# Expert rounds of four subtiles with a merged sixth chunk, transposes behind the down projection

## The chip, the cores and the metric

One core of a Trainium2 chip runs the whole kernel in float32. The metric is the device time of one launch in microseconds (us), the median of the runs shown. All other times come from one profiled execution of the kernel.

## The reference

The input is `x` of shape (8, 64, 16, 16): 8 images of 256 tokens with 64 channels. An attention block comes first, then a mixture of 8 experts in which each token uses two.

```python
x = x + conv_ref(ln_c(x))                  # kq = w_kq x + b, softmax(kq^T kq), w_o (attn v) + b_o
t = to_tokens(x)                           # 2048 tokens x 64 channels
f = ln_t(t)
probs = softmax(f @ router_w.T)            # 8 experts
gate, e = top_2(probs), renormalised
h = silu(f @ w1[e].T) * (f @ w3[e].T)      # w1, w3: 682 x 64
t = t + sum(gate * (h @ w2[e].T))          # w2: 64 x 682
```

## The kernel before, in words

**Attention.** The images go through TensorE (PE), ScalarE (ACT) and VectorE (DVE) one after another. Behind each image DVE chooses the two experts of each token, PE ranks the tokens within their expert (`rank`), and GpSimd (POOL) scatters normalised rows of 128 tokens to a list per expert in HBM (`scatter_row`, four indirect DMAs an image, 32 in all). `t_deviation(b + 1)`, two small POOL instructions that DVE's `normalise_t(b + 1)` needs, is issued ahead of the last row that POOL scatters in its loop turn for image b.

**Subtiles.** The lists are cut into 39 subtiles of 128 rows of one expert (`NS`). Which expert and which rows a subtile has is known only at run time: DVE works out a `table` in three phases (slots 0 to 7, 8 to 15, 16 to 38). Its pieces (`owners_of_slots`, `rows_of_slots`, `used_up`, `subtiles_of_experts`, `occupancy`) stand between DVE's multiplications of the first rounds, in an order written by hand (`tables_between`).

**Rounds.** A round has two subtiles (`HALVES`), so there are 20 rounds (`NT`). For each subtile SP reads expert and row number from the table into registers, and issues a load of the rows (`x_in`, 32.5 KB) and a load of the expert's weights (576 KB). Weights have 8 slots and rows 8. DVE copies rows into `x_pairs` (`pair_up`), PE transposes them (`turn_x`, L962) and ACT copies them to `x_cols` (`columns`). The 682 hidden units are 6 chunks of 128, the last one padded. One `up` step does two chunks: w1 in the upper 64 rows of the array (L982) and w3 in the lower (L984) side by side, into 512 columns of a PSUM bank each. ACT takes the Silu of the first (`silu`, L493), DVE multiplies (`multiply`, L798), and `down` (L1000) adds the six chunks up, the two subtiles in the two column halves of the array. `y_copy` (ACT), `turn_y` (PE, L1011) and `results` (DVE, L806) turn the outcome round, and POOL scatters it to HBM (`scatter_result`, L352).

**Order on PE** in a round i: two up steps, the transposes of the rows of round i + 1 and of the results of round i - 2, the third up step, and then the down steps of round i - 1. The down projection is thus one round behind. An `up` step g waits for `silu` g - 2 and `multiply` g - 3, because there are two banks for w1 and three for w3.

**Order on POOL**: 26 rows are scattered at once, the last six in pairs ahead of rounds 0 to 2, and results are scattered two or three in a round.

**The end.** When all 39 results have landed, they are loaded (`y_in`), weighted, added, transposed with the residual and stored.

Of the kernel before, what the change touches and what calls it, by code (L numbers as in the profile page):

```python
# [17 lines left out]
P = 128  # L18
# [12 lines left out]
HALVES = 2  # L31
PAIR = HALVES * SUB
CAP = B * N
NS = E + (K_TOP * CAP - 1) // SUB
NT = -(-NS // HALVES)
# [9 lines left out]
CHUNKS = -(-H // P)  # L45
HP = CHUNKS * P
WW = HP + CHUNKS * C
STEPS = CHUNKS // 2
PARK = K_TOP * CAP
YROWS = PARK + NS * SUB  # L50
WSLOTS = 8
XRING = 8
RING = 8
ROWS_AT_ONCE = TPB * K_TOP * 6 + 2
ROWS_OF_ROUND = (2, 2, 2)
assert ROWS_AT_ONCE + sum(ROWS_OF_ROUND) == TPB * K_TOP * B
HRING = 2 * STEPS
# [3 lines left out]
def metaformer(nc, x_tok, projections, value_output, b_o, experts, xs, ys, out):  # L61
    with ExitStack() as ctx:
# [6 lines left out]
        bank = [ctx.enter_context(nc.psum_tensor(f"bank{i}", [P, BLK], F32)) for i in range(8)]  # L69
# [78 lines left out]

        x_in = sb("x_in", [P, XRING, HALVES, RW])
        x_pairs = sb("x_pairs", [P, 2, HALVES, 2, C])  # L150
        x_cols = sb("x_cols", [P, 2, PAIR])
        act_sb = sb("act_sb", [P, 3, BLK])
        hid = sb("hid", [P, HRING, BLK])
        y_cols = sb("y_cols", [P, 2, P])
        y_out = sb("y_out", [P, RING, HALVES, C])
# [39 lines left out]
        x_paired, y_row_ready = sem("x_paired"), sem("y_row_ready")  # L195
# [12 lines left out]
        H1_BANK, H3_BANK, Y_BANK, X_BANK, R_BANK = bank[0:2], bank[2:5], bank[5], bank[6], bank[7]  # L208
        TABLES = 9 + PHASES
        CONST_DMAS = 3  # L210
        PER_TILE = 16 * HALVES

        def halves(i):
            return range(min(HALVES, NS - HALVES * i))

        def live(i, columns):
            n = len(halves(i))
            return columns.rearrange("p (c q) -> p c q", q=PAIR)[:, :, 0:n * SUB]
# [7 lines left out]
        def pairs_of(p):  # L226
            return range(-(-OPENED[p] // HALVES), -(-OPENED[p + 1] // HALVES))
# [7 lines left out]
        def all_scattered(engine):  # L235
            for r in range(RING):
                engine.wait_ge(y_scattered[r], 16 * sum(len(halves(i)) for i in range(r, NT, RING)))
# [13 lines left out]
        def _(sp):  # L251
# [12 lines left out]
            def load_weights(i, owners):  # L264
                if i >= WSLOTS // HALVES:
                    sp.wait_ge(hid_used, STEPS * (i - WSLOTS // HALVES + 1))
                for h in halves(i):
                    s = (HALVES * i + h) % WSLOTS
                    sp.dma_start(weights[:, s, :], experts[bass.ds(owners[h], 1)].rearrange("o p c -> p (o c)")
                                 ).then_inc(w_loaded[s], 16)  # L270

            def owners_of(i):
                return [sp.value_load(table[0:1, 0, HALVES * i + h:HALVES * i + h + 1], min_val=0, max_val=E - 1)
                        for h in halves(i)]

            def rows_of(i):
                return [sp.value_load(table[0:1, 1, HALVES * i + h:HALVES * i + h + 1], min_val=0, max_val=E * CAP - SUB)
                        for h in halves(i)]

            def load_rows(i, at):  # L280
                if i >= XRING:
                    sp.wait_ge(y_row_ready, i - XRING + 1)
                    sp.wait_ge(x_paired, i - XRING + 1)
                for h in halves(i):
                    sp.dma_start(x_in[:, i % XRING, h, :], xs[bass.ds(at[h], SUB), :]).then_inc(x_in_loaded[i % XRING], 16)
# [6 lines left out]
            early_rows = [rows_of(i) for i in range(2)]  # L292
            landed(0)
            for i in pairs_of(0):
                load_rows(i, early_rows[i] if i < 2 else rows_of(i))
                if i > 0:
                    load_weights(i, owners_of(i))
            for p in range(1, PHASES):
                sp.wait_ge(table_ready, p + 1)
                for i in pairs_of(p):  # L300
                    at = rows_of(i)
                    if i == pairs_of(p)[0]:
                        landed(p)
# [11 lines left out]
        def _(pool):  # L315
# [31 lines left out]
            def scatter_result(j):  # L347
                i, h = divmod(j, HALVES)
# [16 lines left out]
            nc.gpsimd.memset(ones[:], 1.0).then_inc(ones_made, 1)  # L365
            nc.gpsimd.memset(upto[:], 1.0).then_inc(ones_made, 1)
# [20 lines left out]
            rows_done, results_done = 0, 0  # L387
            for b in range(B):
                own = range(TPB * K_TOP * b, min(TPB * K_TOP * (b + 1), ROWS_AT_ONCE))
                for n in own:  # L390
# [3 lines left out]
                    rows_done += 1  # L394
            for i in range(NT):
                pool.wait_ge(h1_done, STEPS * i + 1)
                paced = i < len(ROWS_OF_ROUND)
                for n in range(ROWS_OF_ROUND[i] if paced else 0):
                    scatter_row(rows_done)
                    rows_done += 1  # L400
                for n in range(0 if paced else HALVES + i % 2):
                    if results_done < HALVES * (i - 1):
                        scatter_result(results_done)
                        results_done += 1
            for j in range(results_done, NS):
                scatter_result(j)

        @block.scalar
        def _(act):
# [71 lines left out]
            def columns(i):  # L481
# [3 lines left out]
                n = SUB * len(halves(i))  # L485
                nc.scalar.copy(x_cols[:, i % 2, 0:n], X_BANK[:, 0:n]).then_inc(x_cols_ready, 1)

            def silu(g):
                act.wait_ge(h1_done, g + 1)
                if g >= 3:  # L490
                    act.wait_ge(hid_done, g - 2)
                i = g // STEPS
                nc.scalar.activation(live(i, act_sb[:, g % 3, :]), live(i, H1_BANK[g % 2][:]), ACT.Silu  # L493
                                     ).then_inc(silu_done, 1)

            def y_copy(i):
                act.wait_ge(hid_used, STEPS * (i + 1))
                if i >= 2:
                    act.wait_ge(y_turned, i - 1)
                n = C * len(halves(i))  # L500
                nc.scalar.copy(y_cols[0:n, i % 2, :], Y_BANK[0:n, 0:P]).then_inc(y_copied, 1)  # L501

            columns(0)
            for i in range(NT):
                if i >= 2:
                    y_copy(i - 2)
                silu(STEPS * i)
                silu(STEPS * i + 1)
                if i + 1 < NT:
                    columns(i + 1)  # L510
                silu(STEPS * i + 2)
            y_copy(NT - 2)
            y_copy(NT - 1)
# [17 lines left out]
        def _(dve):  # L531
# [224 lines left out]
            def pair_up(i):  # L756
                slot, n = i % XRING, len(halves(i))
                dve.wait_ge(x_in_loaded[slot], PER_TILE * (i // XRING) + 16 * n)
# [4 lines left out]
                own = slice(HALVES * i, HALVES * i + n)  # L763
# [28 lines left out]
            def multiply(g):  # L792
                dve.wait_ge(silu_done, g + 1)
                dve.wait_ge(h3_done, g + 1)
                if g >= HRING:
                    dve.wait_ge(hid_used, g - HRING + 1)
                i = g // STEPS
                nc.vector.tensor_tensor(live(i, hid[:, g % HRING, :]), live(i, H3_BANK[g % 3][:]),  # L798
                                        live(i, act_sb[:, g % 3, :]), ALU.mult).then_inc(hid_done, 1)

            def results(i):
                dve.wait_ge(y_turned, i + 1)
                if i >= RING:
                    dve.wait_ge(y_scattered[i % RING], PER_TILE * (i // RING))
                n = len(halves(i))
# [3 lines left out]
            def tables_between(i, s):  # L809
                if (i, s) == (0, 0):  # L810
                    owners_of_slots(1)
                elif (i, s) == (0, 1):
                    rows_of_slots(1)
                elif (i, s) == (1, 1):
                    used_up(1)
                elif (i, s) == (1, 2):
                    subtiles_of_experts(2)
                elif (i, s) == (2, 1):
                    owners_of_slots(2)
                elif (i, s) == (3, 1):  # L820
                    rows_of_slots(2)
                elif (i, s) == (4, 1):
                    occupancy(2)
                elif (i, s) == (7, 1):
                    gate_shifts()

            for i in range(NT):
                for s in range(STEPS):
                    multiply(STEPS * i + s)
                    if s == 0 and i + 2 < NT:  # L830
                        pair_up(i + 2)
                    tables_between(i, s)
                if i >= 2:
                    results(i - 2)
            results(NT - 2)
            results(NT - 1)
# [13 lines left out]
        def _(pe):  # L850
# [104 lines left out]
            def turn_x(i):  # L955
# [5 lines left out]
                for h in halves(i):  # L961
# [3 lines left out]
            def up(g):  # L965
                i, s = divmod(g, STEPS)
                if s == 0:
                    pe.wait_ge(x_cols_ready, i + 1)
                    for h in halves(i):
                        j = HALVES * i + h  # L970
# [5 lines left out]
                for half in range(2):  # L976
                    at = P * (2 * s + half)
                    for h in halves(i):
                        slot = (HALVES * i + h) % WSLOTS
                        dst = slice(PAIR * half + SUB * h, PAIR * half + SUB * (h + 1))  # L980
                        src = slice(SUB * h, SUB * (h + 1))
                        first_ = nc.tensor.matmul(H1_BANK[g % 2][:, dst], weights[0:C, slot, at:at + P],  # L982
                                                  x_cols[0:C, i % 2, src], start=True, stop=True)
                        second_ = nc.tensor.matmul(H3_BANK[g % 3][:, dst], weights[C:P, slot, at:at + P],  # L984
                                                   x_cols[C:P, i % 2, src], start=True, stop=True)
                first_.then_inc(h1_done, 1)
                second_.then_inc(h3_done, 1)

            def down(g):
                i, s = divmod(g, STEPS)  # L990
                pe.wait_ge(hid_done, g + 1)
                if s == 0 and i >= 1:
                    pe.wait_ge(y_copied, i)
                for half in range(2):
                    chunk = 2 * s + half
                    at = HP + C * chunk
# [82 lines left out]
```

## Time and profile before

| what | value |
|---|---|
| median of 3 timed runs | 199.64 us (199.47 to 201.18) |
| span of the profiled execution | 204.1 us |
| PE busy | 174.5 us |
| DVE, POOL and ACT busy | 106.8, 85.5, 75.3 us |
| moved by DMA | 33.36 MB |

The page gives no other time for the profiled execution than its span from the first instruction to the last, 4.5 us above the median of the timed runs. The DMA share is the mean busy share of 16 engines. The first expert round begins on PE at 73.6 us, and the last down projection ends at 185.8 us.

### The profile page before, as it was taken

How to read it: one execution, taken by the hardware profiler on the slowest of the kernel's cores; microseconds unless marked ns; L12 is line 12 of the kernel's file. 1: busy time of each engine (PE TensorE's matmuls, PEld its weight loads, DVE VectorE, ACT ScalarE, POOL GpSimd, SP SyncE). 2: the span in 40 equal slices, each digit the busy share in tenths (PEclk: the TensorE clock that was granted, in tenths of full speed). 3: DMA queues.
4: the chain of work that ended last, by engine and by line, in shares of the span. 5: the costliest groups of instructions: out<-in, count | busy, mean ns of one | idle time of the engine just before them, and what ended most of it. 6: DMA issues, size and time to landing. Idle time of an engine off the chain costs nothing.

```text
span 204.1 us, 5200 instructions
## 1 busy us (share of the span) xinstructions
PE 174.5 (85%) x1744; PEld 141.7 (69%) x1744; DVE 106.8 (52%) x434; ACT 75.3 (37%) x172; POOL 85.5 (42%) x119
## 2 busy tenths in 40 slices
PE   1599989889899688799999999999999999949043
PEld 1254766756757577688888888888888888837032
DVE  4243345455676768956775554454444454612061
ACT  2255351532521611224444444444444444413002
POOL 3235017655666787403333333333333333553200
PEclk9999999999999999759999999999999999997958
DMA  3999000000045469507777887778878783000144
GB/s 73 324 300 248 0 0 20 16 13 28 8 101 178 140 189 305 189 18 257 256 261 250 263 265 259 262 261 261 270 253 265 260 258 116 13 29 6 53 165 103
DMA packets 21627, 33.36 MB, mean 163 GB/s; under 512 B 9810, under 2 KB 14962, under 8 KB 21602
## 3 DMA queue, kind: packets, MB, share of 16 engines
q1 hardware_dynamic: 18466, 29.90, 46.8%
q0 software_dynamic: 2272, 2.35, 3.5%
q10 hardware_dynamic: 864, 0.79, 1.2%
q8 instruction: 14, 0.23, 0.5%
q14 instruction: 11, 0.09, 0.1%
HBM read 25.90 MB, written 7.13 MB: 162 GB/s over the span
## 4 chain that ended last, share of the span: by engine, by line
PE 68%; POOL 8%; issue 8%; DVE 6%; DMA 4%; ACT 2%; POOLq 1%; SPq 1%; ACTq 0%; DVEq 0%
PE bank L982 26%; PE bank L1000 13%; PE bank L878 6%; POOL xs L343 4%; PE bank L899 4%; PE bank L869 4%; PE bank L863 3%; PE bank L962 3%; PE bank L888 2%; DMA y_in<-ys 2%; PE bank L1045 2%; POOL ys L352 2%; PE bank L984 2%; POOL rstd_t L333 1%; PE bank L856 1%
## 5 line engine op out<-in xcount | busy, mean ns | idle before, releaser
L982 PE MATMUL bank<-x_cols,weights 64*128 64x128 f32 x468 | 67.4, 293 | 1.9 <-DVE hid L798 1.9
L984 PE MATMUL bank<-x_cols,weights 64*128 64x128 f32 x468 | 67.5, 293 | 0.0
L982 PEld LDWEIGHTS bank<-x_cols,weights 64*128 64x128 f32 x468 | 59.0, 198 | 9.1 <-issue 7.2
L352 POOL DMA_INDIRECT ys<-y_out,y_row x39 | 37.3, 957 | 58.0 <-PE bank L982 39.5
L798 DVE TENSOR_TENSOR hid<-bank,act_sb 128x512 f32<-128x512 f32 (+1 forms) x60 | 40.5, 676 | 38.6 <-ACT act_sb L493 33.7
L984 PEld LDWEIGHTS bank<-x_cols,weights 64*128 64x128 f32 x468 | 59.0, 198 | 0.0
L493 ACT ACTIVATE act_sb<-bank 128x512 f32<-128x512 f32 (+1 forms) x60 | 35.1, 586 | 57.9 <-PE bank L982 57.5
L343 POOL DMA_INDIRECT xs<-xrows,pos x32 | 31.9, 998 | 22.0 <-issue 10.1
L1000 PE MATMUL bank<-hid,weights 128*64 128x128 f32 x468 | 32.9, 286 | 3.0 <-ACT y_cols L501 3.0
L1000 PEld LDWEIGHTS bank<-hid,weights 128*64 128x64 f32 x468 | 27.9, 143 | 5.6 <-issue 3.4
L899 PE MATMUL bank<-u_sb,probsT 128*128 128x73 f32 x64 | 15.6, 423 | 3.5 <-ACT probsT L446 3.5
L899 PEld LDWEIGHTS bank<-u_sb,probsT 128*128 128x128 f32 x64 | 14.3, 329 | 4.1 <-ACT probsT L446 4.1
L878 PE MATMUL bank<-kq 32*128 32x256 f32 x32 | 16.6, 670 | 0.0
L878 PEld LDWEIGHTS bank<-kq 32*128 32x128 f32 x32 | 9.3, 319 | 4.1 <-issue 1.9
L869 PEld LDWEIGHTS bank<-wu_x,xT 65*128 65x128 f32 x32 | 7.4, 321 | 6.0 <-issue 5.7
L1045 PE MATMUL bank<-ident,total_y 128*128 128x128 f32 x16 | 3.9, 423 | 8.0 <-DVE total_y L846 8.0
L962 PE MATMUL bank<-ident,x_pairs 128*128 128x128 f32 x39 | 9.4, 323 | 0.1
L564 DVE TENSOR_REDUCE neg_max<-bank 128x2 f32<-128x512 f32 x8 | 5.5, 691 | 7.4 <-PE bank L878 7.2
L1045 PEld LDWEIGHTS bank<-ident,total_y 128*128 128x128 f32 x16 | 3.3, 292 | 8.7 <-DVE total_y L846 8.3
L869 PE MATMUL bank<-wu_x,xT 65*128 65x81 f32 x32 | 9.1, 438 | 0.3 <-DVE wu_x L742 0.3
L863 PE MATMUL bank<-xT,proj 64*32 64x256 f32 x16 | 8.5, 631 | 1.0 <-ACT xT L421 1.0
L501 ACT COPY y_cols<-bank 128x128 f32<-128x128 f32 (+1 forms) x20 | 5.3, 263 | 10.8 <-PE bank L1000 6.9
(137 smaller groups left out, 182.1 us busy)
## 6 DMA issues: line engine op xcount, KB each, us to landing
weights<-experts SPq DMA_DIRECT2D x39, 576.0 KB
xs<-zeros SPq DMA_DIRECT2D x4, 1040.0 KB, 10.7
x_in<-xs SPq DMA_DIRECT2D x39, 32.5 KB, 2.8
ys<-y_out,y_row POOLq DMA_INDIRECT x39, 3.9
xs<-xrows,pos POOLq DMA_INDIRECT x32
y_in<-ys SPq DMA_DIRECT2D x2, 256.0 KB, 4.3
y_in<-ys ACTq DMA_DIRECT2D x2, 256.0 KB, 4.6
x_sb<-x_tok SPq DMA_DIRECT2D x1, 384.0 KB, 3.9
```

Of the source, the lines that this page charges most:

```text
L343: nc.gpsimd.indirect_dma_start(xs, bass.IndirectOffsetOnAxis(ap=pos[:, b, at:at + 1], axis=0), xrows[:, TPB * b + at // K_TOP, at % K_TOP, ...
L352: nc.gpsimd.indirect_dma_start(ys, bass.IndirectOffsetOnAxis(ap=y_row[:, j:j + 1], axis=0), y_out[:, i % RING, h, :], None).then_inc(y_sca ...
L493: nc.scalar.activation(live(i, act_sb[:, g % 3, :]), live(i, H1_BANK[g % 2][:]), ACT.Silu).then_inc(silu_done, 1)
L798: nc.vector.tensor_tensor(live(i, hid[:, g % HRING, :]), live(i, H3_BANK[g % 3][:]), live(i, act_sb[:, g % 3, :]), ALU.mult).then_inc(hid_ ...
L863: nc.tensor.matmul(K_BANK[0:CK, 0:N], wk, xT[0:C, b % 2, :], start=True, stop=True).then_inc(kq_done, 1)
L869: ins = nc.tensor.matmul(U_BANK[:, UX * i:UX * (i + 1)], xT[:, b % 2, P * i:P * (i + 1)], wu_x[:], start=True, stop=True)
L878: ins = nc.tensor.matmul(S_BANK[b % 2][:, N * i:N * (i + 1)], kq[:, b % 3, P * i:P * (i + 1)], kq[:, b % 3, :], start=True, stop=True)
L899: ins = nc.tensor.matmul(O_BANK[:, (TX + 1) * i:(TX + 1) * (i + 1)], probsT[:, b % 2, j, P * i:P * (i + 1)], u_sb[:, 2 * b + j, 0:TX + 1], ...
L962: ins = nc.tensor.transpose(X_BANK[:, P * h:P * (h + 1)], x_pairs[:, i % 2, h, :, :], ident[:])
L982: first_ = nc.tensor.matmul(H1_BANK[g % 2][:, dst], weights[0:C, slot, at:at + P], x_cols[0:C, i % 2, src], start=True, stop=True)
L984: second_ = nc.tensor.matmul(H3_BANK[g % 3][:, dst], weights[C:P, slot, at:at + P], x_cols[C:P, i % 2, src], start=True, stop=True)
L1000: ins = nc.tensor.matmul(Y_BANK[C * h:C * (h + 1), 0:P], weights[:, slot, at:at + C], hid[:, g % HRING, src], start=(chunk == 0), stop=(ch ...
```

## The change

- A round has four subtiles (`QUAD`): 10 rounds, the last of three subtiles. There are 12 weight slots (3 rounds) in place of 8 (4 rounds), and four deep rings of four for rows and results.
- An up step does one chunk for four subtiles. There are five full chunks and a sixth step for the 42 hidden units left: w3 and w1 of these lie side by side in one weight block of 106 columns, which stands in both row halves, so that one matmul a subtile computes both, for two subtiles at a time. Silu and multiplication of that step use 42 partitions, and the rest of `hid` is cleared by POOL at the start. The weights of a subtile have 1130 columns in place of 1152.
- On PE the down projection of a round follows its own up steps; behind it come the transposes of the results of the round before and of the rows two rounds ahead. In the last round the results of round 8 are transposed behind its first up step.
- `pair_up(i + 2)` stands behind the third multiplication of a round, `results(i - 2)` behind the first. The pieces of the table are spread over the steps of rounds 0 and 1.
- POOL scatters all 32 rows, then all results in order, with no pacing.

```diff
@@ pool
-                own = range(TPB * K_TOP * b, min(TPB * K_TOP * (b + 1), ROWS_AT_ONCE))
+                own = range(TPB * K_TOP * b, TPB * K_TOP * (b + 1))
                 for n in own:
                     if n == own[-1] and b + 1 < B:
                         t_deviation(b + 1)
                     scatter_row(n)
-            for i in range(NT):
-                pool.wait_ge(h1_done, STEPS * i + 1)
...
-            for j in range(results_done, NS):
+            for j in range(NS):
                 scatter_result(j)
@@ scalar
+                else:
+                    act.wait_ge(h3_done, g + 1)
+                    nc.scalar.activation(act_sb[0:TAIL, g % 3, :].rearrange("p (k n) -> p k n", k=2),
+                                         TAIL_BANKS[C:C + TAIL], ACT.Silu).then_inc(silu_done, 1)
...
             columns(0)
+            for i in range(NQ):
                 silu(STEPS * i)
+                if i == 0:
+                    columns(1)
+                for s in range(1, STEPS):
+                    silu(STEPS * i + s)
+                if i + 2 < NQ:
+                    columns(i + 2)
+                y_copy(i)
@@ vector
+            for i in range(NQ):
                 for s in range(STEPS):
                     multiply(STEPS * i + s)
+                    if s == 0 and i >= 2:
+                        results(i - 2)
+                    if s == 1 and i == NQ - 1:
+                        results(i - 1)
+                    if s == 2 and i + 2 < NQ:
                         pair_up(i + 2)
                     tables_between(i, s)
+            results(NQ - 1)
@@ tensor, up
+                    if s < FULL:
+                        first_ = nc.tensor.matmul(H1_BANK[g % 2][:, src], weights[0:C, slot, P * s:P * (s + 1)],
                                                   x_cols[0:C, i % 2, src], start=True, stop=True)
+                        second_ = nc.tensor.matmul(H3_BANK[g % 3][:, src], weights[C:P, slot, P * s:P * (s + 1)],
                                                    x_cols[C:P, i % 2, src], start=True, stop=True)
+                    else:
+                        rows_ = slice(C * (h % 2), C * (h % 2 + 1))
+                        ins = nc.tensor.matmul(TAIL_BANKS[0:TAIL_W, h % 2, SUB * (h // 2):SUB * (h // 2 + 1)],
+                                               weights[rows_, slot, TAIL_AT:TAIL_AT + TAIL_W], x_cols[rows_, i % 2, src],
+                                               start=True, stop=True)
@@ tensor, down and order
+                for s in range(STEPS):
+                    pe.wait_ge(hid_done, STEPS * i + s + 1)
+                    for h in members(i):
...
             turn_x(0)
             attend(B - 1)
+            for i in range(NQ):
+                up(STEPS * i)
+                if i == 0:
+                    rank(B - 1)
+                    pe.wait_ge(t_ready, B)
+                    turn_x(1)
+                if i == NQ - 1:
+                    turn_y(i - 1)
+                for s in range(1, STEPS):
+                    up(STEPS * i + s)
+                down(i)
+                if 1 <= i < NQ - 1:
+                    turn_y(i - 1)
+                if i + 2 < NQ:
+                    turn_x(i + 2)
+            turn_y(NQ - 1)
```

## Rows read from the trace of the kernel before

**Rows 1.** The page: busy time by engine; one group of DMA issues.

```profile
PE 174.5 (85%) x1744; PEld 141.7 (69%) x1744; DVE 106.8 (52%) x434; ACT 75.3 (37%) x172; POOL 85.5 (42%) x119
...
x_in<-xs SPq DMA_DIRECT2D x39, 32.5 KB, 2.8
```

**Rows 2.** Chain that ended last, by time: start us, us, what.

```profile
105.00 1.46 PE bank L1000 x24
106.46 0.30 PE bank L982
...
110.01 1.46 PE bank L1000 x24
```

**Rows 3.** PE timeline of a steady round: start us, us, instruction.

```profile
123.42 0.44 PE L962 MATMUL bank<-ident,x_pairs 128*128 128x128 f32 x2
...
123.90 0.37 PE L982 MATMUL bank<-x_cols,weights 64*128 64x128 f32 x1
...
124.11 0.27 PE L982 MATMUL bank<-x_cols,weights 64*128 64x128 f32 x1
...
124.78 0.27 PE L982 MATMUL bank<-x_cols,weights 64*128 64x128 f32 x1
...
124.99 1.53 PE L1000 MATMUL bank<-hid,weights 128*64 128x128 f32 x24
```

**Rows 4.** ACT timeline, steady rounds; in brackets idle time and its releaser.

```profile
95.76 0.60 ACT L493 ACTIVATE act_sb<-bank 128x512 f32<-128x512 f32 x1 [1.47 <-PE bank L982]
...
123.52 0.60 ACT L493 ACTIVATE act_sb<-bank 128x512 f32<-128x512 f32 x1 [0.30 <-PE bank L982]
124.01 0.37 ACT L486 COPY x_cols<-bank 128x256 f32<-128x256 f32 x1
126.28 0.60 ACT L493 ACTIVATE act_sb<-bank 128x512 f32<-128x512 f32 x1 [1.90 <-PE bank L982]
...
171.45 0.60 ACT L493 ACTIVATE act_sb<-bank 128x512 f32<-128x512 f32 x1 [1.87 <-PE bank L982]
...
175.20 0.60 ACT L493 ACTIVATE act_sb<-bank 128x512 f32<-128x512 f32 x1 [0.71 <-PE bank L982]
```

**Rows 5.** Windows: length, busy of each engine, clock, DMA share, GB/s.

```profile
82.00:88.00 6.00, 4.60 (x44) 3.88 (x43) 5.43 (x23) 2.05 (x4) 1.92 (x2) 0.68 0.43 154
88.00:94.00 6.00, 6.00 (x71) 5.32 (x71) 2.71 (x9) 2.03 (x5) 0.95 (x1) 0.75 0.28 80
```

**Rows 6.** PE timeline in round 0.

```profile
84.27 0.55 PE L982 MATMUL bank<-x_cols,weights 64*128 64x128 f32 x1 [1.40 <-DVE hid L798]
```

**Rows 7.** POOL timeline: rows of image 6.

```profile
75.56 0.96 POOL L343 DMA_INDIRECT xs<-xrows,pos  x1 [0.30 <-issue]
76.93 0.24 POOL L330 TENSOR_SCALAR variance_t<-moments_t 128x2 f32<-128x2 f32 x1 [0.41 <-issue]
```

**Rows 8.** DVE timeline, from the last image into round 0.

```profile
78.01 0.60 DVE L611 TENSOR_SCALAR xrows<-rows,moments_t,rstd_t 128x128 f32<-128x128 f32 x2 [0.46 <-POOL rstd_t L333]
...
81.97 0.16 DVE L657 TENSOR_SCALAR given<-ends 128x8 f32<-128x8 f32 x1
...
83.43 0.69 DVE L798 TENSOR_TENSOR hid<-bank,act_sb 128x512 f32<-128x512 f32 x1
...
85.28 1.29 DVE L798 TENSOR_TENSOR hid<-bank,act_sb 128x512 f32<-128x512 f32 x2
```

**Rows 9.** SP timeline: first rows of phase 1; weight loads of a steady round.

```profile
86.68 2.00 SPq L285 DMA_DIRECT2D x_in<-xs  x2
...
121.69 0.85 SPq L269 DMA_DIRECT2D weights<-experts  x2
...
126.75 0.85 SPq L269 DMA_DIRECT2D weights<-experts  x2
```

**Rows 10.** POOL timeline at the end.

```profile
188.08 0.95 POOL L352 DMA_INDIRECT ys<-y_out,y_row  x1 [0.30 <-issue]
189.34 0.96 POOL L352 DMA_INDIRECT ys<-y_out,y_row  x1 [0.30 <-issue]
```

More of the change, by code:

```diff
@@ L236, in all_scattered @@
             for r in range(RING):
-                engine.wait_ge(y_scattered[r], 16 * sum(len(halves(i)) for i in range(r, NT, RING)))
+                engine.wait_ge(y_scattered[r], 16 * sum(len(members(i)) for i in range(r, NQ, RING)))
         def load_results(engine, q):
@@ L803, in results @@
                 if i >= RING:
[L804 to L805 removed]
+                    dve.wait_ge(y_scattered[i % RING], 16 * sum(len(members(k)) for k in range(i % RING, i, RING)))
+                n = len(members(i))
                 nc.vector.tensor_copy(y_out[:, i % RING, 0:n, :], R_BANK[:, 0:C * n].rearrange("p (h c) -> p h c", c=C)
@@ L975, in up @@
                     pe.wait_ge(hid_done, g - 2)
[L976 to L982, printed above, removed]
+                for h in members(i):
+                    slot = (QUAD * i + h) % WSLOTS
+                    src = slice(SUB * h, SUB * (h + 1))
+                    if s < FULL:
+                        first_ = nc.tensor.matmul(H1_BANK[g % 2][:, src], weights[0:C, slot, P * s:P * (s + 1)],
@@ L986, in up, with down @@
                 first_.then_inc(h1_done, 1)
                 second_.then_inc(h3_done, 1)
[L989 to L992, printed above, removed]
+            def down(i):
+                if i >= 1:
                     pe.wait_ge(y_copied, i)
-                for half in range(2):
-                    chunk = 2 * s + half
-                    at = HP + C * chunk
-                    for h in halves(i):
-                        slot = (HALVES * i + h) % WSLOTS
-                        src = slice(PAIR * half + SUB * h, PAIR * half + SUB * (h + 1))
-                        ins = nc.tensor.matmul(Y_BANK[C * h:C * (h + 1), 0:P], weights[:, slot, at:at + C],
-                                               hid[:, g % HRING, src], start=(chunk == 0), stop=(chunk == CHUNKS - 1))
+                else:
+                    pe.wait_ge(hid_cleared, 1)
+                for s in range(STEPS):
+                    pe.wait_ge(hid_done, STEPS * i + s + 1)
+                    for h in members(i):
+                        slot = (QUAD * i + h) % WSLOTS
+                        at = SUB * h if s < FULL else tail_at(h)
+                        ins = nc.tensor.matmul(Y_BANK[C * (h % 2):C * (h % 2 + 1), P * (h // 2):P * (h // 2 + 1)],
+                                               weights[:, slot, HP + C * s:HP + C * (s + 1)], hid[:, i % 2, s, at:at + SUB],
+                                               start=(s == 0 and h < 2), stop=(s == STEPS - 1), skip_group_check=True)
```

226 lines of the change are left out of this document (102 added, 124 removed).

## The prediction

> **What bounds the kernel now.** I read the page first: PE is busy for 174.5 of 204.1 us [rows 1]. The chain of waits that ended last then shows where: from about 91 to 177 us the same round repeats every 5.01 us, from one down projection at 105.00 to the next at 110.01, all of it PE [rows 2]. So the middle is PE's own length. Before it, from 76 to 91 us, PE waits for DVE and POOL, and its granted clock is at the lower level (1.2 GHz, window means 0.68 and 0.75) [rows 5]. Behind it a tail from the last result scatter at 189.34 to the end takes 14.8 us [rows 10]. I price the three parts: the start up to where round 2 of the changed kernel begins on PE, seven steady rounds, and round 9 with the tail.
>
> **A steady round on PE.** An up slot (one pass of a w1 and a w3 matmul side by side) takes 0.112 us: six from 124.11 to 124.78. A switch between kinds of matmul costs about 0.1 more: 0.21 from 123.90 to 124.11, and again from 124.78 to 124.99. Three transposes with their switch take 0.48 (123.42 to 123.90) [rows 3]. A down projection of two subtiles takes 1.46 [rows 2]. Today four subtiles take 96 slots' worth in two rounds, 2 x 24 x 2 passes over two row halves, which is 48 slots side by side: 2 x 5.01 = 10.02 us in all. Changed: the merged chunk halves the slots of the sixth chunk, so 44; 44 x 0.112 + 0.2 for both switches = 5.1; down 2 x 1.46 = 2.9; six transposes 0.48 + 3 x 0.14 = 0.9. Sum 8.9, a gain of 1.1 in a round, of which 0.45 is the merged chunk and the rest switches. That is PE with no wait.
>
> **What the cover was and what is gone.** Today the down projection is a round behind, so no Silu is urgent. After the change all of them are.
> - In the up steps: Silu g starts as step g ends (123.52, 0.3 after the start of its last slot, which stands a switch ahead of 123.42), takes 0.60 [rows 3, 4], and step g + 2 waits for it. Start to start, a step takes 8 x 0.112 = 0.89; from the start of g to the end of Silu g are 0.89 + 0.16 + 0.04 + 0.60 = 1.7, and weights are loaded 0.1 before the matmul. Two steps take 1.78, so this is a tie; I take 0.2 a round for it.
> - SP: today it issues two weight loads at 121.69 and the next two at 126.75, four register reads and four loads between, with a wait of some 0.2 to 0.7 [rows 9]. For four subtiles that is 9.0 to 9.6 us of work. It is prefetched, so it doesn't add to PE's time, but a round can't be much shorter than 9.1.
> - In the down projection: its sixth step needs Silu and multiplication of the merged chunk, which ends just ahead of it. Steps 0 to 4 cover 5/6 x 2.9 = 2.4 us. Needed are 0.60 (Silu), 0.69 (multiplication [rows 8]) and 0.2 to 0.3 of signals: 1.5. If ACT hears of the matmuls at once, that is covered.
> - But the trace says that it hears late. The third up step of a round ends at 124.78 + 0.27 = 125.05, right ahead of the down projection, and its Silu begins at 126.28, though ACT is free from 124.38 [rows 3, 4]: 1.2 us late. All 16 rounds with a third Silu from 95.76 to 171.45 show it, by 0.7 to 1.4 us; the next, at 175.20, when no weight load is left in flight, is prompt [rows 4]. Steps that are followed by up steps or transposes are heard of at once (123.52). Today that hides behind a round. In the changed kernel the merged step is exactly such a step, with 2.4 us of down steps behind it. Bounds: zero (prompt), and 2.4 (until PE stands still at the sixth step), which gives a stall of 1.5. With a delay as seen, 0.7 to 1.4, the stall is 0 to 0.5; since the stream of down steps is longer than the 1.46 us in which I can see the signal come, I take 0.5.
>
> The Trainium skill, "TensorE: Matmul & The Clock Gate", section "The cost: per-tile semaphore tail", says that increments of matmuls serialise at about 26 ns each; by it alone the two signals of the merged step would be under 0.1 us late, and the round 9.1. The trace disagrees with that where a down projection follows (1.2 us).
>
> So a round: 8.9 + 0.2 + 0.5 = 9.6, bounds 8.9 and 10.5.
>
> **The start.** Three waits are new or longer.
> 1. POOL. Today image 6 scatters only two rows at once, and `t_deviation(7)` follows the first (76.93). Now it follows three: two more scatters of 1.26 us each [rows 7, 10], less the 0.4 that POOL waited. So `normalise_t(7)` comes 2.2 us later than 78.01 [rows 8], and all of DVE behind it.
> 2. DVE and the rows of round 2. `pair_up(2)` now copies slots 8 to 11, which phase 1 of the table opens, and stands behind the third multiplication. Today it copies slots 4 and 5. `owners_of_slots(1)` and `rows_of_slots(1)` take 1.4 and 1.25 us with a 0.6 us multiplication between them (81.97 to 85.28) [rows 8]. With the 2.2 from POOL and no `pair_up(2)` between, the table stands at 87.2. SP then needs 1.3 us for two register reads (86.68) [rows 9], so 2.3 for four, and some 2.3 to issue four loads; the last lands 2.8 after its issue [rows 1]: 94.5. Until then DVE stands still, and multiplications 3 to 5 with `used_up(1)` run to 97.7, the sixth down step to 98.8 at the low clock, four transposes of rows to 99.8. Round 1 begins there.
> 3. DVE in round 1. The phase 2 pieces of the table, about 2.0 and 1.75 us (23 slots instead of 8), stand between multiplications on which PE now waits in the same round. From the first multiplication of round 1 (PE at the low clock, about 102.5): 6 x 0.65 + 2.0 + 1.75 + 0.65 (`pair_up(3)`) = 8.3, and waits of about 1, so the sixth ends at 111.9; then down step 5 and transposes, 1.5. Round 2 begins at 113.4. Bounds: 110.4 if the loads are issued as fast as two are today and the clock is back early, and 115.
>
> Today the same work (8 subtiles up and down) is done at about 103: the round that begins one round ahead of 106.46, at 101.4, has 8 subtiles up and 6 down behind it, and one down projection more is 1.46 [rows 2]. So the start loses 10.
>
> **Round 9 and the tail.** Results of round 7 are copied only behind the first multiplication of round 9, those of round 8 a little later, so POOL has 4 + 4 + 3 scatters left. The first starts 2.65 us into round 9 (up 0.9, Silu, multiplication, copy, 0.3), the eleventh 10 x 1.26 later [rows 10], at 15.25. PE needs only about 9.5 for that round, so its own waits there (the transposes of round 8 wait 1.7 us for the copy of round 7) are hidden behind POOL. From the last scatter to the end I take the 14.8 of today. So 30.0 from the start of round 9 to the end.
>
> **The sum.** 113.4 + 7 x 9.6 + 30.0 = 210.6, against 204.1: 6.5 us more, 3.2%. The profiled execution is 4.5 us above the median of the timed runs; the difference should carry over, so 199.6 + 6.5 = 206.1.
>
> **Rivals.**
> - *Signals prompt.* The round is 9.1: 207.1, or 202.6. For it: at 175.20 the signal is prompt. Against: the 16 rounds with weight loads in flight are not, and the loads fill most of a round (about 8 of 9 us). Chance 0.2.
> - *Signals held until PE stands still*, every round: 10.5, 216.9, or 212.4. For it: in those 16 rounds the signal comes only in the second half of the down projection. Chance 0.2.
> - *Faster.* The merged chunk and fewer switches win: the round is 8.7 (switches cheaper than I take them), and the start costs 3 us less because SP issues four loads as quickly as two. 110.4 + 7 x 8.7 + 30.0 = 201.3, or 196.8. It decides from a round under 8.9 and a start before 111. Against it stands SP's own 9 us for four subtiles. Chance 0.12.
> - *The clock falls.* PE stands still for 1.4 us ahead of 84.27 [rows 6], and the clock is at the lower level for some 7 us around and behind that (0.32 x 6 / 0.5 + 0.25 x 6 / 0.5) [rows 5]. A stall of 1.5 in each round could do that in the steady part. A fall costs 3.4 us; in three of seven rounds, on top of 9.6, some 9: 219, or 215. Chance 0.08.
>
> My forecast, the delay as seen and rounds of 9.3 to 9.9, has 0.4. A measurement of this kernel can tell about 1% from no change. Faster by over 1% is only the third rival, 0.12; within 1% (up to 201.6) are the low ends of the first rival and of the start, 0.18; the rest, 0.70, is slower. The range for 8 in 10 runs from a round of 8.9 with an early start, about 199.5, to rounds held until PE stands still with a late start, 213.5.
>
> **What the profile after would show.** Right: x_pairs of round 2 released by the x_in load at about 94 us; PE idle ahead of that; round starts 9.6 apart; the Silu of 42 partitions 1 us or more behind its matmuls, and PE waiting for hid ahead of the last down step; eleven scatters 1.26 apart at the end. Wrong if rounds come 8.9 apart or less, if the merged Silu is prompt, or if the table of phase 2 doesn't hold round 1 up.

## Result and profile after

The changed kernel takes 205.81 us (median of 6 runs, 204.98 to 206.47), the kernel before 200.73 us (median of 6, 199.47 to 201.18) on the same chip: a ratio of 1.0279, 95% interval 1.0240 to 1.0319, or 5.1 us slower. The forecast was 206.1. The profiled execution of the changed kernel took 204.98 us, with a span of 203.2.

The page of the changed kernel (busy engines, then groups: busy us, mean ns | idle time ahead and what ended it):

```profile
PE 165.1 (81%) x1666; PEld 136.6 (67%) x1666; DVE 103.3 (51%) x404; ACT 74.4 (37%) x153; POOL 86.7 (43%) x120
...
L1014 PE MATMUL psum<-hid,weights 128*64 128x128 f32 x468 | 32.0, 286 | 5.7 <-DVE hid L801 5.3
...
L763 DVE COPY x_pairs<-x_in 128x512 f32<-128x512 f32 (+1 forms) x10 | 4.6, 459 | 11.3 <-DMA x_in<-xs 11.3
```

PE has 9.4 us less to do than in [rows 1], and the kernel is longer: PE now stands still where it didn't. The down projection waits for `hid` (5.3 us), and DVE waits 11.3 us for rows. The timelines of POOL, DVE, SP and PE, from the last image to round 2, show where (start us, us, instruction, idle time in brackets):

```profile
79.11 0.24 POOL L336 TENSOR_SCALAR variance_t<-moments_t 128x2 f32<-128x2 f32 x1
```
```profile
80.19 0.60 DVE L613 TENSOR_SCALAR xrows<-rows,moments_t,rstd_t 128x128 f32<-128x128 f32 x2 [2.31 <-POOL rstd_t L339]
...
87.11 0.17 DVE L686 TENSOR_SCALAR table<-owned 128x8 int32<-128x8 f32 x1
87.19 0.69 DVE L801 TENSOR_TENSOR hid<-psum,act_sb 128x512 f32<-128x512 f32 x1
92.91 0.43 DVE L763 COPY x_pairs<-x_in 128x512 f32<-128x512 f32 x1 [5.03 <-DMA x_in<-xs]
...
124.15 0.60 DVE L763 COPY x_pairs<-x_in 128x512 f32<-128x512 f32 x1 [1.88 <-DMA x_in<-xs]
133.95 0.43 DVE L763 COPY x_pairs<-x_in 128x512 f32<-128x512 f32 x1 [1.02 <-DMA x_in<-xs]
```
```profile
89.67 1.92 SPq L291 DMA_DIRECT2D x_in<-xs  x4
94.01 1.88 SPq L275 DMA_DIRECT2D weights<-experts  x4
98.29 2.02 SPq L291 DMA_DIRECT2D x_in<-xs  x4
...
113.62 2.94 SPq L275 DMA_DIRECT2D weights<-experts  x4
119.02 1.89 SPq L291 DMA_DIRECT2D x_in<-xs  x4
123.31 2.05 SPq L275 DMA_DIRECT2D weights<-experts  x4
127.81 1.89 SPq L291 DMA_DIRECT2D x_in<-xs  x4
```
```profile
94.06 2.92 PE L1014 MATMUL psum<-hid,weights 128*64 128x128 f32 x24 [3.70 <-DVE hid L801]
...
103.81 0.69 PE L994 MATMUL psum<-x_cols,weights 64*106 64x128 f32 x8 [1.24 <-DVE hid L801]
...
107.14 1.25 PE L1014 MATMUL psum<-hid,weights 128*64 128x128 f32 x16 [0.74 <-DVE hid L801]
```

`t_deviation(7)` begins 2.2 us later than in [rows 7], `normalise_t(7)` 2.2 later than in [rows 8]. Then DVE stands still for 5.03 us with multiplications behind it, and PE for 3.70.

A round is best measured at the copy of `x_cols` that opens it, on ACT:

```profile
109.23 0.58 ACT L480 COPY x_cols<-psum 128x512 f32<-128x512 f32 x1 [4.01 <-PE psum L970]
...
114.00 0.60 ACT L488 ACTIVATE act_sb<-psum 128x512 f32<-128x512 f32 x1 [0.35 <-PE psum L988]
114.62 0.60 ACT L492 ACTIVATE act_sb<-psum 42x512 f32<-42x512 f32 x1
118.02 0.58 ACT L480 COPY x_cols<-psum 128x512 f32<-128x512 f32 x1 [2.80 <-PE psum L970]
...
128.69 0.58 ACT L480 COPY x_cols<-psum 128x512 f32<-128x512 f32 x1 [4.68 <-PE psum L970]
```

Rounds 2, 3, 4 are 8.79, 10.67 and 9.10 long. The Silu of 42 partitions starts at 114.62, straight behind the one before it. In round 1, where ACT was free, its delay can be read alone: the matmuls of the merged step end at 103.81 + 0.69 = 104.50, and the Silu starts 0.13 later, where [rows 4] had 1.2 us. Round 9 begins with the first up slot at 172.94:

```profile
104.63 0.59 ACT L492 ACTIVATE act_sb<-psum 42x512 f32<-42x512 f32 x1 [1.43 <-PE psum L994]
```
```profile
172.94 0.37 PE L988 MATMUL psum<-x_cols,weights 64*128 64x128 f32 x1
```

Rounds 2 to 8 run from 109.1 (the copy less 0.1) to 172.9, 63.8 us in all, 9.12 each on average.

The end on POOL, to set beside [rows 10]:

```profile
175.60 0.95 POOL L358 DMA_INDIRECT ys<-y_out,y_row  x1 [3.15 <-DVE y_out L813]
...
188.24 0.96 POOL L358 DMA_INDIRECT ys<-y_out,y_row  x1 [0.31 <-issue]
```

Eleven scatters, 1.26 apart; from the last to the end 15.0.

### The profile page after: what moved, and what is told of

Its sections match the earlier page's. It is cut to its first block, busy times and chain, and to the rows that moved or that the text cites. A ratio compares the mean times of both kernels' runs of the same rounds, so it can differ in the third digit from the quotient of the medians.

```text
span 203.2 us, 4908 instructions
## 1 busy us (share of the span) xinstructions
PE 165.1 (81%) x1666; PEld 136.6 (67%) x1666; DVE 103.3 (51%) x404; ACT 74.4 (37%) x153; POOL 86.7 (43%) x120
## 4 chain that ended last, share of the span: by engine, by line
issue 36%; PE 29%; POOL 24%; DMA 4%; ACT 2%; DVE 2%; POOLq 1%; SPq 1%; DVEq 0%; ACTq 0%
POOL ys L358 17%; PE psum L886 8%; PE psum L907 6%; POOL xs L349 6%; PE psum L877 4%; PE psum L871 4%; PE psum L896 3%; PE psum L1060 2%; DMA y_in<-ys 2%; PE psum L864 2%; ACT probsT L441 1%; DMA ys<-y_out,y_row 1%; POOL rstd_t L339 1%; DMA proj<-projections 1%; POOLq L62 1%
## 5 line engine op out<-in xcount | busy, mean ns | idle before, releaser
L988 PE MATMUL psum<-x_cols,weights 64*128 64x128 f32 x390 | 52.5, 295 | 0.0
L990 PE MATMUL psum<-x_cols,weights 64*128 64x128 f32 x390 | 52.5, 295 | 0.0
L988 PEld LDWEIGHTS psum<-x_cols,weights 64*128 64x128 f32 x390 | 50.1, 204 | 2.1 <-issue 2.0
L801 DVE TENSOR_TENSOR hid<-psum,act_sb 128x512 f32<-128x512 f32 (+1 forms) x50 | 33.2, 673 | 33.6 <-ACT act_sb L488 32.0
L990 PEld LDWEIGHTS psum<-x_cols,weights 64*128 64x128 f32 x390 | 50.1, 204 | 0.0
L488 ACT ACTIVATE act_sb<-psum 128x512 f32<-128x512 f32 (+1 forms) x50 | 29.3, 586 | 24.4 <-PE psum L988 24.1
L1014 PE MATMUL psum<-hid,weights 128*64 128x128 f32 x468 | 32.0, 286 | 5.7 <-DVE hid L801 5.3
L1014 PEld LDWEIGHTS psum<-hid,weights 128*64 128x64 f32 x468 | 26.7, 141 | 9.8 <-DVE hid L801 6.5
L907 PE MATMUL psum<-u_sb,probsT 128*128 128x73 f32 x64 | 15.6, 423 | 3.5 <-ACT probsT L441 3.5
L907 PEld LDWEIGHTS psum<-u_sb,probsT 128*128 128x128 f32 x64 | 14.4, 329 | 4.1 <-ACT probsT L441 4.1
L886 PE MATMUL psum<-kq 32*128 32x256 f32 x32 | 16.6, 669 | 0.0
L886 PEld LDWEIGHTS psum<-kq 32*128 32x128 f32 x32 | 9.3, 319 | 4.1 <-issue 1.9
L763 DVE COPY x_pairs<-x_in 128x512 f32<-128x512 f32 (+1 forms) x10 | 4.6, 459 | 11.3 <-DMA x_in<-xs 11.3
```

Source lines behind the costliest of these rows:

```text
L801: nc.vector.tensor_tensor(live(i, hid[:, i % 2, s, :]), live(i, H3_BANK[g % 3]), live(i, act_sb[:, g % 3, :]), ALU.mult).then_inc(hid_done, 1)
L886: ins = nc.tensor.matmul(S_BANK[b % 2][:, N * i:N * (i + 1)], kq[:, b % 3, P * i:P * (i + 1)], kq[:, b % 3, :], start=True, stop=True)
L907: ins = nc.tensor.matmul(O_BANK[:, (TX + 1) * i:(TX + 1) * (i + 1)], probsT[:, b % 2, j, P * i:P * (i + 1)], u_sb[:, 2 * b + j, 0:TX + 1], ...
L988: first_ = nc.tensor.matmul(H1_BANK[g % 2][:, src], weights[0:C, slot, P * s:P * (s + 1)], x_cols[0:C, i % 2, src], start=True, stop=True)
L990: second_ = nc.tensor.matmul(H3_BANK[g % 3][:, src], weights[C:P, slot, P * s:P * (s + 1)], x_cols[C:P, i % 2, src], start=True, stop=True)
L1014: ins = nc.tensor.matmul(Y_BANK[C * (h % 2):C * (h % 2 + 1), P * (h // 2):P * (h // 2 + 1)], weights[:, slot, HP + C * s:HP + C * (s + 1)] ...
```

## Experiments

The kernels ran in three groups, each on one chip beside the kernel before, whose medians were 200.55 us (the first four below), 199.72 (the next four) and 200.01 (the last four); ratios are to it. Unless said otherwise the edit is to the changed kernel.

**The kernel before, profiled again.** No edit.

> The kernel before, unchanged, profiled once more. Its profiled execution above had a span of 204.1 us, 4.5 above the timed median, while the changed kernel's had 203.2 at a time of 204.98. Theory: the first profile was of an untypically long execution, so the changed kernel's loss of 5 us doesn't show as a difference of the two spans; this one has a span near 199, and the steady round stays 5.0 us. The late third Silu (0.7 to 1.4 us behind its matmuls) is then either gone or still there; if it is still there the signal delay belongs to the kernel. Rival: the span is again about 204, and the timed difference lies outside the spans.

Measured: 199.86 us, span 198.1, not 204.1. Its ACT timeline and the windows that answer to [rows 5]:

```profile
91.59 0.37 ACT L486 COPY x_cols<-bank 128x256 f32<-128x256 f32 x1
92.67 0.60 ACT L493 ACTIVATE act_sb<-bank 128x512 f32<-128x512 f32 x1 [0.71 <-PE bank L982]
...
97.68 0.60 ACT L493 ACTIVATE act_sb<-bank 128x512 f32<-128x512 f32 x1 [0.71 <-PE bank L982]
```
```profile
82.00:88.00 6.00, 5.74 (x58) 4.96 (x59) 5.45 (x21) 1.83 (x5) 1.91 (x2) 1.00 0.14 40
88.00:94.00 6.00, 6.00 (x95) 5.28 (x91) 4.76 (x16) 2.57 (x6) 1.92 (x2) 1.00 0.58 194
```
```profile
183.10 0.95 POOL L352 DMA_INDIRECT ys<-y_out,y_row  x1 [0.30 <-issue]
```

The third Silu of a round is prompt in this execution (0.71 of idle, not 1.90), the clock doesn't fall at 84, and the last scatter comes 6.2 us earlier than in [rows 10], a shift in two parts. The round is the same, but ahead of it are 2.3 us less and behind it 3.6 less. Those 3.6 begin with one more late copy on ACT: in the first execution the results of the last but one down projection, which ends at about 180.1, were copied only here. PE stood still for 2.97 us instead of 0.46, and its next 12 down matmuls took 2.75 us instead of 1.50, with a granted clock of 0.72 from 182 to 188.

```profile
182.65 0.27 ACT L501 COPY y_cols<-bank 128x128 f32<-128x128 f32 x1 [3.61 <-remote]
```

The timed executions of the kernel before that ran beside the last four kernels had spans from 197.6 to 199.5 us. So the execution on which the forecast was built was about 6 us longer than a usual one, and the late signals came with that execution, not with the program. Against this one the changed kernel's 203.2 is 5.1 longer, as in the medians.

**`t_deviation(7)` one row earlier.**

```diff
-                    if n == own[-1] and b + 1 < B:
+                    if n == (own[1] if b == B - 2 else own[-1]) and b + 1 < B:
```

> The changed kernel with t_deviation(7) put ahead of the second row that POOL scatters for image 6, where it stood before, all else as it is. Theory (three waits add up at the start): normalise_t(7) comes about 2.2 us earlier, the table of phase 1 too, and with it the whole of rounds 0 to 9: 2 to 2.5 us less, ratio to the kernel before about 1.017. Rival (the rows of round 2 land when the loads let them, or a later wait takes the place of this one): under 0.8 us less, ratio 1.024 or more.

Measured: 204.6 us, 1.0183 [1.0104, 1.0262]; 1.2 us less between the medians, 1.9 by the ratios. That lies between theory and rival, and the two intervals overlap, so this run alone doesn't settle the term. In its trace round 1 opens at 96.65 instead of 97.83, but round 2 at 108.70 instead of 109.23: a part of the gain is lost again in waits behind it. That some of it is real shows below, where the same edit takes another 1.4 us off the version with early results.

**Rows of round 2 copied last in round 0.**

```diff
-                    if s == 2 and i + 2 < NQ:
+                    if s == (5 if i == 0 else 2) and i + 2 < NQ:
```

> The changed kernel with pair_up(2) behind the sixth multiplication of round 0 in place of the third, so that DVE doesn't stand still with three multiplications of the round behind it. Theory: the down projection of round 0 is done at about 91 us, the transposes wait for the rows alone, round 1 begins 2.5 to 3 us earlier; ratio about 1.015. Rival: the table pieces of phase 2 on DVE set the start of round 2 anyway, and the gain is under 1 us: ratio 1.023 or more.

Measured: 205.83 us, 1.0278 [1.0219, 1.0337]: nothing, although round 1 opens at 94.81 instead of 97.83. Round 1 gives back more than that, and round 2 opens 1.9 us later than in the changed kernel (DVE, then PE):

```profile
104.24 0.43 DVE L763 COPY x_pairs<-x_in 128x512 f32<-128x512 f32 x1 [3.59 <-DMA x_in<-xs]
```
```profile
105.39 0.66 PE L1014 MATMUL psum<-hid,weights 128*64 128x128 f32 x8 [2.44 <-DVE hid L801]
107.63 1.97 PE L1014 MATMUL psum<-hid,weights 128*64 128x128 f32 x16 [1.58 <-DVE hid L801]
```

DVE now waits for the rows of round 3, which SP issues at 98.67: not earlier, since they stand behind the weights of round 2. The clock adds to it: behind PE's waits of 2.44 and 1.58 us the granted clock from 106 to 112 was 0.54, and 16 down matmuls took 1.97 us, where the changed kernel's took 1.25. The rounds behind are shorter in return: from the copy ahead of round 2 to that ahead of round 8 pass 54.1 us instead of 55.5.

**No merged chunk** (six full chunks, no `TAIL`).

> The changed kernel without the merged chunk: six full chunks, 1152 weight columns, everything else as it is. Theory (PE's length sets the steady round): 4 more slots of 0.112 us in a round, so 0.45 more a round in eight rounds, 3 to 4 us more in all, ratio 1.043 to 1.048. Rival (rounds wait for rows, SP or signals, and the saved slots are spent waiting): under 1.5 us more, ratio under 1.036.

Measured: 208.56 us, 1.0413 [1.0342, 1.0483]; 2.7 us more than the changed kernel. Its undisturbed rounds are 9.24 or 9.25 long against 8.79: 0.45 each, as the slots say. In the trace, though, only 0.9 us of the loss stands between the openings of rounds 2 and 8, because DVE's waits for rows shrink as PE's round grows; 1.9 stand between the openings of rounds 0 and 2, where the clock was low for longer (0.67 from 94 to 100 and 0.76 from 100 to 106, against 0.72 and 1.00). The merged chunk does what it should on PE; the loss is elsewhere.

**Results of round i-1 copied within round i.**

```diff
                 for s in range(1, STEPS):
                     up(STEPS * i + s)
+                    if s == 1 and i >= 1:
+                        turn_y(i - 1)
...
-                    if s == 0 and i >= 2:
-                        results(i - 2)
-                    if s == 1 and i == NQ - 1:
+                    if s == 1 and i >= 1:
                         results(i - 1)
```

> The changed kernel with the transposes of the results of round i - 1 behind the second up step of round i, in every round, and their copy behind the second multiplication, so that POOL scatters a round earlier. Theory (the tail is POOL's: eleven scatters of 1.26 us left when round 9 begins): seven are left instead, PE doesn't wait 1.6 us in round 9, and the last scatter starts 3 to 4 us earlier; ratio about 1.011. Rival (the loss is all at the start, and the tail follows PE): under 1.2 us less, ratio 1.022 or more.

Measured: 203.57 us, 1.0161 [1.0100, 1.0222]; 2.3 us less, where 3.4 had been expected. POOL has seven scatters left in round 9 instead of eleven, and from the `x_cols` copy that opens round 8 to the end pass 35.2 us instead of 38.5. Against it each round is 9.08 instead of 8.79 long, because the transposes of results now stand alone between up steps: the rows of PE show 0.1 us more ahead of them, 0.1 in them and 0.1 behind them.

**SP: rows of round i+1 ahead of the weights of round i.**

```diff
+                load_rows(quads_of(p)[0], at)
                 for i in quads_of(p):
+                    if i + 1 in quads_of(p):
+                        load_rows(i + 1, rows_of(i + 1))
                     load_weights(i, owners_of(i))
```

> The changed kernel with SP's order turned round within a phase of the table: the loads of rows of round i + 1 ahead of the weight loads of round i. Theory (rows land late because they queue on SP behind four reads, four weight loads and their data): DVE's wait for the rows of round 5 (1.9 us at 124 us) goes, and the waits of 0.7 to 1.0 us in the rounds behind it; 1.5 to 2 us less in the time, since only the first reaches PE; ratio about 1.019. Rival (SP's total work of some 9 us a round is the limit, whatever its order): the time stays, ratio 1.025 or more.

Measured: 208.59 us, 1.0456 [1.0380, 1.0531]: 2.8 us more, not less (its four runs spread from 206.44 to 210.81; without the longest it is 2.2 more). DVE waits for no rows in the steady rounds, but PE waits for weights (SP, then PE):

```profile
111.26 6.23 SPq L291 DMA_DIRECT2D x_in<-xs  x8
119.90 1.88 SPq L275 DMA_DIRECT2D weights<-experts  x4
```
```profile
129.91 0.34 PE L989 MATMUL psum<-x_cols,weights 64*128 64x128 f32 x1 [1.19 <-DMA weights<-experts]
```

The weights of round 4 are issued 6.3 us later than at 113.62. The lateness has moved, so it is not the order that is short but SP's time. (The profiled execution was the shortest of the four, 206.44 us, and 1.5 us longer than that of the changed kernel; what made the others longer wasn't seen.)

**Rows of round 2 late, and SP's order**, together.

> e3 and e6 together: pair_up(2) behind the sixth multiplication of round 0 and rows ahead of weights on SP. In e3 round 1 began 3.0 us earlier but DVE then waited 3.6 us for the rows of round 3. Theory: with the rows of round 3 issued first that wait goes, and the 3 us of e3 come out: 4.5 to 5 us less than the changed kernel, ratio 1.003 to 1.006. Rival (the table pieces on DVE set the start of round 2): no more than e6 alone gives.

Measured: 205.26 us, 1.0233 [1.0164, 1.0302]: 0.5 us less than the changed kernel, where 4.5 to 5 had been expected. PE waits 1.89 us for weights at 107.33 and DVE 4.67 us for rows at 116.32.

**All four edits.**

> All four: t_deviation(7) early, pair_up(2) late, rows ahead of weights, results a round earlier. Theory: 2 + 3 + 1.8 + 3.5 us, some 10 us less than the changed kernel and 5 less than the kernel before: ratio 0.970 to 0.980. Rival: the start is held by the table pieces on DVE and the tail by PE and the last scatters, so half of it is lost: ratio 0.99 to 1.00.

Measured: 199.82 us, 0.9993 [0.9961, 1.0026]: the kernel before, to within the measurement. The theory had 0.970 to 0.980; what came is its rival, 0.99 to 1.00, with much of the gain lost.

**SP reads four values a round instead of eight.** A row number holds its expert, so SP divides the register that it has.

```diff
                     load_rows(i, at)
-                    load_weights(i, owners_of(i))
+                    load_weights(i, [a // CAP for a in at])
```

> The changed kernel, but from round 2 on SP doesn't read the expert of a subtile out of the table: it divides the row that it has read already (row // 2048), so a round has four register reads instead of eight. Theory (SP sets the pace of the changed kernel): from one x_in load to the next weight load SP takes 4.3 to 4.5 us, half of it for four reads; without four of the eight reads a round of SP is about 6.5 us, the waits of DVE for x_in (1.88, 1.02, 0.88, 0.75, 0.95) are gone, every steady round is 8.8, and the kernel is 2.7 us faster: about 203.1. Rival (the rows land late because their packets stand behind those of the weights in the DMA queues): the waits stay near 1 us each and the time stays at 205.8. Rival (the forecast's own: PE's round is 8.9 with no wait): gain of 1 us at most.

Measured: 203.24 us, 1.0127 [1.0070, 1.0184]; 2.6 us less (forecast 2.7). SP, then DVE:

```profile
109.97 1.93 SPq L291 DMA_DIRECT2D x_in<-xs  x4
112.50 2.02 SPq L275 DMA_DIRECT2D weights<-experts  x4
117.00 2.51 SPq L291 DMA_DIRECT2D x_in<-xs  x4
```
```profile
123.20 0.42 DVE L763 COPY x_pairs<-x_in 128x512 f32<-128x512 f32 x1
131.99 0.42 DVE L763 COPY x_pairs<-x_in 128x512 f32<-128x512 f32 x1
```

From rows to weights SP takes 2.5 us instead of 4.3, the waits of DVE in the steady rounds are gone (the one in round 0 stays), and the `x_cols` copies of rounds 2 to 8 come 8.79, 8.78, 8.79, 8.79, 8.78 and 8.68 apart: every round is PE's own length. So SP's time is what had to give.

The rival, rows held up behind the data of weights, isn't ruled out by this, since rows that are issued earlier arrive earlier either way. The changed kernel's trace speaks for a share of it: in the start, with the DMA engines busy for 0.12 of the time from 88 to 94, the last rows were there 1.3 us after the four issues (91.59 to 92.91); in the steady rounds, with 0.81 from 120 to 130, it was 3.2 us (120.91 to 124.15) and 4.3 (129.70 to 133.95). With 1.3 us there too, neither wait would have been there: DVE had asked at 122.27 and 132.93. SP's pace and the slower landing make the wait together. No run takes the landing apart from the rest.

**`t_deviation(7)` early and results early.**

> t_deviation(7) behind the second row of image 6, and the results of round i-1 copied within round i, together, SP's order and the place of the rows' copy as in the changed kernel. If the two gains add (1.9 and 2.3 us): 201.6. If both only make room for the same wait of DVE for rows that SP issues late: 203.5, as with one of them alone.

Measured: 202.14 us, 1.0071 [1.0033, 1.0108]; 3.7 us less: the two gains add (1.2 and 2.3 by the medians; by the ratios 1.9 and 2.4 against 4.2).

**The same, and four reads less on SP.**

> The kernel before this one in the list, and the expert taken from the row as in the first of the list. If SP sets the pace: 201.6 - 2.7 = 198.9, faster than the kernel before the change by under 1%. If the rows are late for another reason: 201.6.

Measured: 200.46 us, 1.0009 [0.9977, 1.0041]; 1.7 us less than without, where 2.7 were expected. With results early a round of PE is 9.08, so SP's 8.7 to 9.7 was mostly hidden already: in the steady rounds DVE had waited only 1.70 and 0.46 us for rows.

**The same, and the rows of round 2 late.**

> As the third of the list, and the rows of round 2 copied behind the sixth multiplication of round 0, where they gained nothing alone, because the rows of round 3 then came late (3.59 us of waiting in round 1). With four reads less ahead of them the rows of round 3 are issued about 94.4 instead of 98.7 and land by 99, when DVE asks for them: round 1 begins 3 us earlier and is no longer. If SP sets the pace: 195.5 to 196.5, 2 to 2.5% faster than the kernel before the change. If the copy only moves the wait again (as it did alone): 198.9.

Measured: 197.76 us, 0.9867 [0.9816, 0.9919]. This is the fastest version: 1.3% below the kernel before, 3.9% below the changed one. The late copy, worth nothing alone, is worth 2.7 us here, because the rows of round 3 now come in time but for 1.70:

```profile
95.85 1.92 SPq L291 DMA_DIRECT2D x_in<-xs  x4
```
```profile
101.71 0.43 DVE L763 COPY x_pairs<-x_in 128x512 f32<-128x512 f32 x1 [1.70 <-DMA x_in<-xs]
...
104.36 0.68 DVE L801 TENSOR_TENSOR hid<-psum,act_sb 128x512 f32<-128x512 f32 x1
```
```profile
105.10 1.74 PE L1012 MATMUL psum<-hid,weights 128*64 128x128 f32 x16 [1.58 <-DVE hid L801]
```

It stayed 1.3 us above its forecast. In the profiled execution (199.42 us, the longest of the six) round 1 is still 14.1 long: the table of phase 2 holds the fifth multiplication until 104.36, PE waits for it, and the granted clock from 103 to 109 is 0.72.

## Why the prediction was right, and where it wasn't

The time was right within 0.3 us and the sign for the stated reason (the start loses more than the rounds gain). But that closeness is partly luck. The difference was forecast at 6.5 us and measured at 5.1; the base, taken as 199.6 from three runs, came out at 200.7 from six and hid most of that. And inside the difference the terms were off on both sides and cancelled.

- **Start.** Forecast 113.4, bounds 110.4 to 115; measured 109.1, outside them. POOL's 2.2 us and the table at 87.2 were right to 0.1. The rows were there at 92.9, not 94.5: four loads are issued in 1.92 us, and the last is there 1.3 after that; I had put 2.3 and the whole 2.8 of the page one behind the other. Round 1 then took 11.4, not 13.6. The table of phase 2 does hold it, as forecast, but for 1.24 and 0.74 us of PE: I had put all of DVE's work in a row from a late first multiplication, and that multiplication came at 99.61, not behind 102.5.
- **Steady round.** Forecast 8.9 + 0.2 + 0.5 = 9.6; measured 9.12. PE's own part is 8.79, and 8.35 for the last, which has no rows left to transpose. The 0.2 for the Silu tie is nothing: with SP out of the way every round is 8.79. The 0.5 for the late signal is nothing: the signals are prompt in the changed kernel, and in a second execution of the kernel before. My main case fails in the step that took the delay of one execution for a property of the kernel; a prompt merged Silu was the sign of being wrong that I had named myself. The rival *signals prompt*, which had 0.2, is right about the signals. Its round of 9.1 is right by luck: its 0.2 for the Silu tie isn't there, and what is there instead is the wait for rows. The Trainium skill, "TensorE: Matmul & The Clock Gate", section "The cost: per-tile semaphore tail", has increments serialise at about 26 ns each. These later traces agree that the delay is small, though they don't resolve 26 ns: the merged Silu of round 1 starts 0.13 us after its matmuls (104.50 to 104.63).
- **SP.** The step "prefetched, so it doesn't add to PE's time" was wrong, though the number beside it (no round much under 9.1) was right. SP's chain of reads and issues, 8.7 to 9.7 us from one round's `x_in` loads to the next, is as long as a round, so prefetching never gets ahead. With the slower landing it costs 2.9 us in seven rounds (63.8 against 61.0 from 110.1 to 171.1 in the kernel with four reads), of which 1.88 in round 3; that is 0.4 a round, about what I had given to signals. Four reads less gave back 2.6 us.
- **Tail.** Forecast 30.0 from the start of round 9; measured 203.2 - 172.9 = 30.3. First scatter 2.7 into the round (2.65), ten pitches of 1.26, 15.0 behind (14.8). Right.
- **The base.** The sum was made against an execution of 204.1; a usual one is 198.1. From 210.6 to 203.2 the after side shrank by 7.4: 4.3 at the start and 3.4 in the rounds, with 0.3 more at the end. The before side shrank by 6.0: 2.3 at the start and 3.6 behind the rounds. Hence a difference of 5.1 where I had 6.5. The step "the difference should carry over" did hold in size, but not by its parts. Against the usual execution (eight subtiles done at 103 less the 2.3 that its down projections come earlier, 100.6) the start loses 109.1 - 100.6 = 8.5, not 10; seven rounds gain 14 x 5.01 - 63.8 = 6.3, not 3; and the tail loses 30.3 - (198.1 - 170.7) = 2.9, where my sum had today's tail at 204.1 - 173.1 = 31.0 and so saw no loss. Sum 5.1.
- **Other rivals.** Held signals (10.5) and a falling clock in steady rounds did not occur: windows from 110 to 173 have a granted clock of 1.00. *Faster* asked for a start before 111 and a round under 8.9; the start was there, and the round too once SP read less. The 201.3 that it came to is even the span of that kernel (201.4), and still that kernel is slower than the kernel before (1.0127): what the rival had wrong was the 204.1 to compare with, of which 3.6 us behind the rounds and 2.3 in the start were not usual.

## What to carry to other kernels

Before a term is built on a delay, look whether a second execution shows it too; one profile can be 3% long, and its peculiarities enter both the base and the forecast. When a pipeline's rounds get bigger and the distance between making and using shrinks, check every queue that feeds it for its own length of a round, register reads included: a prefetcher as slow as the round never gets ahead, and every delay in landing then shows. Measure that landing where the other loads are in flight, not in a quiet stretch. A copy moved later only pays if the loads behind it in the queue come in time as well, so try such edits together, not only one by one.

## What was not expected of the hardware

- The same program ran once with third Silus 0.7 to 1.4 us late in 16 rounds [rows 4] and once with none late. The first also copied one result 2.5 us late at its end. What made the difference stays open.
- A register read on SP costs as much as a DMA issue. With four reads between them, weights follow rows by 4.3 us; without, by 2.5 (1.9 of them the four issues): some 0.45 us a read, an estimate from two traces, against 0.48 an issue.
- TensorE's clock in the start of the changed kernel: behind PE's wait of 3.70 us ahead of 94.06 it was granted 0.72 on the mean of 6 us, so for a part of them the lower level (1.2 GHz); the wait of 1.24 us ahead of 103.81 left it at full speed. In the fastest version the lower level came behind waits of 1.10, 0.56 and 1.58 us, in the kernel before behind one of 1.40 in one execution [rows 6]. Which waits cost clock can't be told from these rows. The windows of the changed kernel:

```profile
94.00:100.00 6.00, 5.94 (x66) 5.22 (x68) 3.19 (x12) 1.65 (x4) 0.00 (x0) 0.72 0.82 269
100.00:106.00 6.00, 4.76 (x82) 4.46 (x80) 5.47 (x17) 2.79 (x5) 0.00 (x0) 1.00 0.78 261
```
